# A delta-rule scan with four operations a chunk, its working tiles in SBUF, and a new order of steps around it

## What is computed

```python
x = _layernorm(x + _L0_attn_ref(...))      # causal attention, 16 heads of 8
x = _layernorm(x + _L0_ffn_ref(...))       # soft mixture of experts
x = _layernorm(x + _L1_attn_ref(...))      # gated delta rule, then a SiLU-gated MLP
x = _layernorm(x + _L1_ffn_ref(...))       # scaled ternary MLP with four layers

def step(Sm, inp):                          # delta rule, one token, per head: state 8 x 8
    qi, ki, vi, bi = inp
    Sk = jnp.einsum('bhkv,bhk->bhv', Sm, ki)
    upd = ki[..., :, None] * (vi - Sk)[..., None, :]
    Sm = Sm + bi[..., None, None] * upd
    oi = jnp.einsum('bhkv,bhk->bhv', Sm, qi)
    return (Sm, oi)
...
h = hidden_states + o @ Wo
y = rmsnorm(h, ln2)
h = h + jax.nn.silu(y @ Wg) * (y @ Wu) @ Wd
...
h = jax.nn.silu(_tlin(x, w1_w, w1_s)) * _tlin(x, w2_w, w2_s)
h = jax.nn.gelu(_tlin(h, h1_w, h1_s), approximate=False)
h = jax.nn.gelu(_tlin(h, h2_w, h2_s), approximate=False)
return _tlin(h, w3_w, w3_s)
```

## Time and profile before

| | us |
|---|---|
| runs | 1367.09, 1373.09, 1374.86; median 1373.09 |
| the profiled execution, its own time | 1367.92 |
| its span | 1366.2 |
| busy in the span: PE, DVE, ACT, POOL | 1170.0, 926.2, 623.3, 453.3 |
| the chain that ended last: PE, DVE, ACT, POOL | 50%, 25%, 10%, 4% of the span |
| HBM over the span | 57 GB/s |

### The profile page before, as it was taken

How to read it: one execution, slowest core, us unless ns; L and a number is a source line. 1 busy time by engine, 2 the same in 40 slices (tenths; PEclk the granted TensorE clock), 3 DMA queues, 4 the chain that set the end, 5 groups by cost and what they waited for, 6 DMA issues and landing times.

```text
span 1366.2 us, 19874 instructions
## 1 busy us (share of the span) xinstructions
PE 1170.0 (86%) x6173; PEld 616.5 (45%) x6173; DVE 926.2 (68%) x2401; ACT 623.3 (46%) x1194; POOL 453.3 (33%) x466
## 2 busy tenths in 40 slices
PE   5989889999899998989896751178999999999997
PEld 2434355453554544635444430134555545455453
DVE  3536536657587677776775577988988988898321
ACT  2071743736737447375373410213464454545642
POOL 3031311212333143232333233236446445544510
PEclk8999999999999999999999885579999999999999
DMA  3212030130321414114213168121020220200000
GB/s 99 82 47 71 1 109 9 48 94 33 109 65 42 131 32 134 47 29 138 55 35 67 25 149 200 48 49 44 14 65 19 47 65 8 57 24 8 24 8 8
DMA packets 85756, 79.91 MB, mean 58 GB/s; under 512 B 42800, under 2 KB 63408, under 8 KB 83632
## 3 DMA queue, kind: packets, MB, share of 16 engines
q1 hardware_dynamic: 85680, 79.01, 21.6%
HBM read 43.17 MB, written 35.00 MB: 57 GB/s over the span
## 4 chain that ended last, share of the span: by engine, by line
PE 50%; DVE 25%; ACT 10%; issue 9%; POOL 4%; DMA 1%; SPq 0%; ACTq 0%; DVEq 0%; POOLq 0%
PE ps L1305 10%; PE ps L954 5%; PE ps L1288 5%; DVE arena L1808 4%; ACT arena L1442 4%; PE ps L991 4%; PE ps L923 4%; ACT arena L1404 3%; PE ps L957 3%; PE ps L964 3%; PE ps L980 2%; DVE arena L2075 2%; PE ps L1058 2%; DVE ps L2070 2%; DVE arena L2073 2%
## 5 line engine op out<-in xcount | busy, mean ns | idle before, releaser
L1808 DVE TENSOR_REDUCE arena<-ps 128x4 f32<-128x512 f32 (+2 forms) x192 | 197.8, 1044 | 89.4 <-PE ps L957 86.3
L1305 PE MATMUL ps<-arena,late 128*128 128x512 f32 x512 | 224.5, 592 | 0.0
L1404 ACT ACTIVATE arena<-ps 128x512 f32<-128x512 f32 (+2 forms) x200 | 109.7, 567 | 232.6 <-PE ps L923 105.4
L1442 ACT ACTIVATE arena<-ps 128x1024 f32<-128x1024 f32 (+3 forms) x256 | 169.9, 711 | 30.6 <-PE ps L980 29.5
L753 POOL TENSOR_SCALAR_AFFINE_SELECT arena<-arena 128x512 f32<-128x512 f32 x128 | 82.9, 650 | 291.9 <-ACT arena L1442 290.4
L964 PE MATMUL ps<-mask_qk,ident_b 128*128 128x512 bf16 x505 | 137.6, 390 | 31.2 <-DVE arena L2087 31.1
L1305 PEld LDWEIGHTS ps<-arena,late 128*128 128x128 f32 x512 | 96.2, 190 | 115.8 <-issue 114.1
L1591 ACT ACTIVATE arena<-ps,f_s 128x512 f32<-128x512 f32 x128 | 85.2, 688 | 102.9 <-PE ps L1305 93.9
L1288 PE MATMUL ps<-arena,late 128*128 128x512 f32 x256 | 116.6, 609 | 7.8 <-ACT arena L1591 7.3
L848 POOL TENSOR_TENSOR arena<-arena 128x512 f32<-128x512 f32 x64 | 81.7, 1276 | 120.8 <-DVE slot_T L2104 76.5
L1404 ACT ACTIVATE arena<-ps,arena 128x128 f32<-128x128 f32 (+1 forms) x128 | 62.3, 528 | 124.5 <-DVE arena L1835 49.3
(11 more groups left out here) (186 smaller groups left out, 1960.7 us busy)
## 6 DMA issues: line engine op xcount, KB each, us to landing
qr<-q_rep SPq DMA_DIRECT2D x8, 1024.0 KB, 5.6
kr<-k_rep SPq DMA_DIRECT2D x8, 1024.0 KB, 7.9
scan_d<-late SPq DMA_DIRECT2D x56, 138.0 KB, 3.0
arena<-scan_d SPq DMA_DIRECT2D x12, 552.0 KB, 7.2
q_rep<-hilo SPq DMA_DIRECT2D x24, 256.0 KB, 3.3
k_rep<-hilo SPq DMA_DIRECT2D x24, 256.0 KB, 3.8
proj_d<-arena SPq DMA_DIRECT2D x8, 768.0 KB, 5.1
late<-proj_d SPq DMA_DIRECT2D x8, 768.0 KB, 4.5
```

The costliest lines, as they stand in the source:

```text
L1305: last = pe.matmul(ps[:, ring2.bank(f"{n}{c}"), :], w[:, k, c * P:(c + 1) * P], src[:, k, :], start=(k == 0), stop=(k == HC - 1))
L1404: return act.activation(dst, src(ps[:, bank, :]), func, **kw)
L1442: act.activation(prob[:, gg % 2, 2 * pr:2 * pr + 2, p_off[jt]:p_off[jt] + w], ps[:, bank:bank + 2, 0:w], ACT.Exp).then_inc(p_taken, 1)
L1808: v.tensor_reduce(heads[:, 2 * pr:2 * pr + 2, gs[0]:gs[-1] + 1], ps[:, at:at + 2, 0:len(gs) * w].rearrange("p q (n w) -> p q n w", w=w), X ...
```

## The change

1. **Four operations a chunk.** `w_s` and `k_u` become two tiles of a quarter each, with one column more: column HD of a row of `w_s` holds minus v, written by ACT ahead of time (`negate_v`, four activations of 128 elements a tile, semaphore `v_negated`); column CH of a row of `k_u` is the state. So the sum over nine terms, negated, is v minus w times state, and the sum over five is the new state. Subtraction and addition are gone.
2. **All in SBUF.** `live` is that column of `k_u` (a stride of five words) and `live_u` a tile of the arena; neither is in PSUM.
3. **Joint roots.** The root for h of one tile and that for x4 of another are taken in one sequence of eight operations on 2 x 4 values (`roots`).
4. **New order.** DVE: the sums of the second half come before `add_x4`, with two scan operations behind each; `AT_Y, AT_H, AT_X, AT_S = 4, 28, 56, 52`; in step 1 norm_x3 stands at operation 56 of the scan. ACT: `square_h` before `apply_x4`, hT's copy before those of m; in the last scan step the last history after x3T. PE: `project_o` after the first quarter of m instead of the second, `turn_h` after the third instead of the fourth, `turn_x3` after two of the four token groups of `last_out`, the three idle matmuls behind it gone; fewer idle matmuls in step 1.

The core of the diff:

```diff
-        live = [ps[:, 6 + k, 0:QUARTER * HD * HD].rearrange("p (c v d) -> p c v d", v=HD, d=HD) for k in range(2)]
-        live_u = [ps[:, 6 + k, QUARTER * HD * HD:QUARTER * HD * (HD + CH)].rearrange("p (c v j) -> p c v j", v=HD, j=CH)
-                  for k in range(2)]
+        live_u = [c2.take(QUARTER, HD, CH) for _ in range(2)]
...
+        w_s = [c2.take(QUARTER * HD, CH, HD + 1) for _ in range(2)]
+        k_u = [c2.take(QUARTER * HD, HD, CH + 1) for _ in range(2)]
+        live = [tile[:, :, :, CH].rearrange("p (c v) d -> p c v d", v=HD) for tile in k_u]
+        v_neg = [tile[:, :, :, HD].rearrange("p (c v) j -> p c v j", v=HD) for tile in w_s]
+        st_both = slot_T[:, 256:256 + 64].rearrange("p (k a b) -> p k a b", k=2, a=8)
...
+            def negate_v(t, h, q):
+
+                act.wait_ge(sc_loaded[h], CREDIT + (t - h) * 16 + 48)
+                wc = s_wu[h].rearrange("p (c j) w -> p c w j", j=CH)
+                act.activation(v_neg[q % 2], wc[:, q * QUARTER:(q + 1) * QUARTER, HD:2 * HD, :], ACT.Copy, scale=-1.0) \
+                    .then_inc(v_negated, 1)
...
-                    yield o.mark(v.tensor_reduce(now_u[:, at, :, :], w_s, X, ALU.add))
-                    yield o.mark(v.tensor_tensor(now_u[:, at, :, :], wc[:, c, :, HD:2 * HD].rearrange("p j v -> p v j"),
-                                                 now_u[:, at, :, :], ALU.subtract))
-                    yield o.mark(v.tensor_tensor(k_u, now_u[:, at, :, :].unsqueeze(2).broadcast_to([P, HD, HD, CH]),
+                    yield o.mark(v.tensor_reduce(now_u, w_s[half][:, rows, :, :], X, ALU.add, negate=True))
+                    yield o.mark(v.tensor_tensor(k_u[half][:, rows, :, 0:CH], now_u.unsqueeze(2).broadcast_to([P, HD, HD, CH]),
...
-                    yield o.mark(v.tensor_reduce(ku_sum, k_u, X, ALU.add))
...
-                    yield o.mark(v.tensor_tensor(after[:, (c + 1) % QUARTER, :, :], now[:, at, :, :], ku_sum, ALU.add))
+                    yield o.mark(v.tensor_reduce(after[:, (c + 1) % QUARTER, :, :], k_u[half][:, rows, :, :], X, ALU.add))
...
+            def roots(t, which):
+
+                o = Order(v, h_done, DVE_H, t, CREDIT)
+                rsqrt(o, which(3), which(2), which(4))
                 o.end('DVE_H')
...
-AT_Y, AT_N, AT_H, AT_S = 4, 18, 34, 84
+AT_Y, AT_H, AT_X, AT_S = 4, 28, 56, 52
...
-DVE_SCAN = 6 * NC
+DVE_SCAN = 4 * NC
```

More of the change, by code:

```diff
@@ L318, in build @@
         x2t = [c2.take(4, D) for _ in range(2)]
-        w_s = c2.take(HD, CH, HD)
-        k_u = c2.take(HD, HD, CH)
-        ku_sum = c2.take(HD, HD)
         bn2 = c2.take(4, 6)
@@ L1288, in by_hidden, with by_token @@
                 return pe.matmul(ps[:, ring2.bank(use), :], w, src, start=True, stop=True)
-            def by_token(use, turn, hid, w, done, first):
+            def by_token(use, turn, hid, w, done, first, beside=None):
                 ring2.wait_free(pe, use, *turn)
                 for j in range(4):
+                    if j == 2 and beside is not None:
+                        beside()
                     for c in range(HC):
@@ L1380, in _ @@
             now = step(0, None, 1, {})
-            now = step(1, 0, 0, now)
+            now = step(1, 0, 0, now, 2, 3)
             with pe.Fori(0, 2) as i:
@@ L1641, in keep_history, with step @@
                 act.activation(u_c[h][:, cs, :, :], live_u[q % 2], ACT.Copy).then_inc(hist_kept, 1)
-            def step(scanned, mlp, last, done, h):
+                if q < 2:
+                    negate_v(t, h, q + 2)
+                elif more:
+                    negate_v(t + 1, 1 - h, q - 2)
+            def step(scanned, mlp, last, done, h, more=True):
                 if last is not None:
@@ L1668, in step @@
                     take_n(last, 1)
-                if scanned is not None:
-                    keep_history(scanned, h, 3)
+                if scanned is not None and last is not None:
+                    keep_history(scanned, h, 3, more)
                 if last is not None:
@@ L2157, in step @@
                 further(DVE_SCAN)
-                if mlp is not None:
-                    norm_x3(mlp, 1 - h, order(ln3_done, DVE_LN, mlp, False))
+                if mlp is not None and not early_x3:
+                    norm_x3(mlp, 1 - h, Order(v, ln3_done, DVE_LN, mlp, CREDIT))
             step(0, None, None, 0)
-            step(1, 0, None, 1)
+            step(1, 0, None, 1, True)
             step(2, 1, None, 0)
```

127 lines of the change are left out of this document (70 added, 57 removed).

## The result

The changed kernel takes **1408.85 us** in the median of its runs (1407.95 to 1409.37), before it takes 1373.29: a ratio of 1.0276 (95% interval 1.0251 to 1.0301). It is slower, as forecast, but by 35.6 us and not by 10. The profiled execution has a span of 1406.7 us against 1366.2, so 40.5 us are to be explained. All of them lie in part two, which begins at 844.6 us in both, and most in the middle of it. The stretches that answer to the earlier trace rows, each from the last layer's gates to the next (ahead of the first, the start): us, PE, PEld, DVE, ACT, POOL busy, granted clock of PE, DMA, GB/s.

The account below looks back on a forecast made before the run. Part two was taken as a DVE chain to about 1262 us, then a PE chain. Terms -7.6 + 10.7 + 8 - 1.3 = +9.8 us gave 1377.7 profiled, median 1383 us; range 1380 to 1398, eight in ten 1352 to 1398.

Parts of the forecast that it names:

- The port: DVE operations with two SBUF operands contend with POOL; each long POOL operation meeting a scan multiplication costs +0.52 us.
- the stride: Scan's multiplication reading live at every fifth word: 0.10 us each, +1.6 us a step; bounds 0 and 0.17 us.
- the new wait: DVE's first-half sums, now after 13 of 16 chunks, wait 3.4 us for POOL's first pair of products.
- start, up to the first gates: Part two before the last layer's first gates: removed operations and fewer waits outweigh port and stride, -7.6 us.
- first full step: First full step of part two gives back the start's gain, 63.3 us against 52.6: +10.7 us.
- step without a scan: Step set by PE, with no fillers and no stop: -1.3 us.
- meetings: Scan multiplications on DVE meet eleven of POOL's 18 long operations: +5.7 us a step, bounds 0 and 14.
- new waits, net: DVE's waits: 3.4 us for products, 1.0 for a history copy and project_o, less 2.0 of old waits: +2.4 a step.
- the root at +19.6: DVE's root for h should end 19.6 us into the step, after 31 scan operations of 0.49 us.
- its chain of 15.9 us: From h's root through POOL, hT's transposes, layer m's last quarter and gates to the first product pair, at +35.5.
- the port hardly bites: Rival: multiplications barely meet POOL's bursts, PE becomes the bound at 51.7 us a step; about 1353 us, chance 0.24.
- the strides are free: Rival: port bites but strided reads cost nothing; middle step 54.2 us, total +4, 1377 us, chance 0.28.

Follow-up runs that it names:

- e2: Changed kernel, but the w multiplication reads 64 side-by-side constants instead of the strided state column (values wrong): 1383.76 us.
- e6: Changed kernel, but PE transposes h after layer m's last quarter, as before the change: 1403.73 us.
- e18: e14 plus x4's norm on ACT moved behind the copies of the gates; port still there: 1392.45 us.
- e17: e15 plus x4's norm on ACT moved behind the copies of the gates: 1366.51 us.
- e3: Changed kernel with u and w of the scan in PSUM (port off), ACT copying w there; state stride kept: 1379.54 us.
- e9: e3 and e6 together: u and w in PSUM, h's transposes after layer m's last quarter on PE: 1380.11 us.
- e14: e6 plus ACT's copy of hT moved back behind layer m's four copies: 1413.38 us.
- e15: e9 plus ACT's copy of hT moved back behind layer m's four copies: 1390.22 us.
- e11: e5 with h's root earlier, after 30 of 96 scan operations instead of 42: 1372.81 us.
- e10: e3 and e7 together: u and w in PSUM, h's root after 20 scan operations: 1359.44 us.
- e7: Changed kernel, but DVE takes up h's residual and joint root after 20 scan operations instead of 28: 1398.45 us.
- e5: Changed kernel with the old six-operation scan, live and u in PSUM; prices the new order alone: 1396.57 us.
- e13: e10, but in step 1 x3's norm stands behind the scan again, as before the change: 1360.42 us.
- e19: Changed kernel, but the w multiplication reads constants at hops of two words in quarters 0 and 2, four in the others: 1397.65 us.

## Why the prediction was wrong

The direction was right and the time was outside the range, 1408.9 us against 1383 and at most 1398. The port, the stride and the new wait are real, each shown above; their sizes and what they hang on were not as forecast. The sum by steps, forecast and measured:

| | forecast | measured |
|---|---|---|
| start, up to the first gates | -7.6 | +0.8 |
| first full step | +10.7 | +13.9 |
| five middle steps | +8 | +27.6 |
| step without a scan | -1.3 | -1.7 |
| end | 0 | -0.1 |
| sum | +9.8 | +40.5 |

And a middle step, by the terms of the prediction:

| | forecast | measured | from |
|---|---|---|---|
| removed operations | -8.3 | -8.3 | both are gone, forecast's own price |
| longer reductions | +1.6 | +1.5 | (452 - 427 + 488 - 418) x 16 |
| joint root | -1.0 | not taken apart | |
| meetings | +5.7 | +4.2 | 264 x 16 |
| new waits, net | +2.4 | +4.7 | 4.0 - 1.2 and 1.9 |
| stride | +1.6 | +3.3 | (627 - 418) x 16 |
| sum | +2.0 (of 53.4) | +5.5 | 59.2 - 53.7 |

With the forecast's -1.0 for the root, the measured terms add to 4.4 of the 5.5 us; part of the rest (0.7 us) is a four-element operation with two operands in SBUF (1744), 489 ns on average in place of 158 twice a step, up to 1.3 us. The new waits missed by 2.3 us in three parts. The wait for products was 4.0 and not 3.4, the one for history copies 1.9 and not 1.0. And I let 2.0 us of old waits go, from a total over part two, where the middle steps before had 1.2.

**The stride was taken at half its price: the largest single miss.** I chose 0.10 us between 0 and 0.17; it is 0.21 in these traces, and e2 shows it to be the source's hop alone. 0.11 us more on 128 multiplications is 14 us, over half of the 26 that the median lies over the forecast; as an estimate that holds, since in e2 a price of 26 us gave 25. The hop costs 0.8 ns an element. "Vector Engine (DVE) Microarchitecture Reference", 5.2 of the Trainium skill, has 1.73 against 1.05 ns a column for a source that hops 4 KiB at every element: 0.17 us by an estimate from it, nearer than my choice from the 32-element row. The upper end of the range was built on 0.17 too, so it held nothing for a late root or a longer chain.

**The step that failed beside it is the root at +19.6 and its chain of 15.9 us.** The pair was to end at +35.5 and ends at +40.3 on average, 2.8 us by the root and 2.0 by the chain. For the root I took "31 scan operations of 0.49 us"; a quiet chunk takes 2.12 us (1083.57 to 1085.69), 0.53 an operation, and meetings come on top. With the read dense the root comes at 20.7, with the port off at 20.2: its lateness is stride and port once more, through DVE's list. In the chain, "the last quarter of m 3.4" took 4.8 to 6.1 us, because PE ran part of it at 1.2 GHz behind its own stop. That stop was forecast, at 2 us, and nothing was put for what follows it.

That chain was longer than before by plan, with the quarter in it, and taking the quarter out doesn't bring the old 13.6 us back (e6), which the working could not have told: nothing in it followed ACT's list. There x4's norm waits for the joint root, and layer m's copies and two table loads stand behind it. I had costed the negations on ACT and never the *order* there. Three moves together, h's transposes on PE, hT's copy on ACT and x4's norm on ACT, took 16 us off the changed kernel (e18) and 13 with the port off (e17 against e3). Of them the transposes alone gave 5 or nothing (e6, e9), hT's copy on top cost 10 (e14 against e6, e15 against e9), and x4's norm on top gave 21 and 24. x4's norm moved alone was not tried, nor were the joint roots parted again in the new order, so whether that one move would do stays open. An earlier root also helps: 24 us with the old scan (e11), 20 with the port off (e10 against e3), 10 in the changed kernel (e7).

**The start was forecast 7.6 us shorter and came 0.8 longer.** The stride explains 3.5 us of it (32 multiplications more dearly by 0.11). The rest is not taken apart. The first gates come at 945.0 in the changed kernel (forecast: 937), at 943.0 with the root earlier (e7), 941.2 with the read dense (e2), 939.4 with the port off (e3); with the old scan at 945.1 and, with the root earlier, 938.8 (e5, e11).

**The port's size was right in part by luck.** 5.7 us forecast and 4.2 measured looks like a good term. But I priced it as a constant: eleven long operations met, whatever the rest does. Over the kernels in which both multiplications can meet POOL it ran from 4.2 to 9.1 us a step, and it was small in the changed one because DVE stood beside the burst. The rule of the Trainium skill ("SBUF — State Buffer", Who interferes with whom) holds here: with one operand of each in PSUM the 256 multiplications of e3 show no meeting.

**What else held and what didn't.** The step without a scan, the end and the reductions came as forecast. The first full step grew by 13.9 us, not 10.7, but it had no early start to give back; with the port off and the root earlier, 6 us of its length came from x3's place (e13). Of the signs named, DVE's idle (3.4 us) came, and PE's before h's transposes was 3.8 us, not 2. The maximum of a multiplication was 1.74 us, not 1.3. POOL's output products hardly grew, 1302 ns on average over the span against the 1400 that I had put; its gate products took 1366 and 1330 where they had taken 1274 and 1271.

Some of the working's sums are off by little. The chain's terms add to 15.6 and not 15.9 us, 55.4 less 53.7 is 1.7 and not 1.6, the step without a stride price is 53.8 and not 54.2, and 1373 - 21 is 1352.

The rival *the port hardly bites* was priced at 1353 us. e3 is nearest to that case, with the stride and ACT's extra copies: 1379.5, no faster than before, so taking the port away would not have done what the rival says. Only with the root earlier as well does it come to 1359 (e10). The rival *the strides are free* was priced at 1377 us; e2 gives 1383.8.

## What to carry to other kernels

Terms that share one cover don't add. Where an engine can either wait out another's burst or run through it and collide, removing one cost buys the other; measure each part alone *and* both together, since here 29 and 10 us alone made 49. When two results are computed together, look on every engine at what is queued behind the consumer of the one that was not urgent: with x4's norm moved out of the front of ACT's list the chain was 4.6 us shorter (18.8 in e15, 14.2 in e17), more than the 1.0 us that I had expected of the joint root. And keep an operand that is read every few words out of the short chain, or price it from a row with the hop, not between a bound and zero.

## What the runs showed of the hardware

- **A hop of five words costs ScalarE as well.** The history copy of 256 elements took 384 ns from dense PSUM (the first row, before) and 666 from the strided column in SBUF (the second, changed). Two things changed there. The dense copy of u beside it, 128 elements, went from 272 only to 302 when its source moved to SBUF, so my estimate is that over 0.2 us are the hop.

```profile
L1640 ACT ACTIVATE arena<-ps x32: 375/384/415, 861.2 to 1259.0; 128x256 f32<-128x256 f32 x32
```

```profile
L1647 ACT ACTIVATE arena<-arena x32: 646/666/687, 868.5 to 1301.2; 128x256 f32<-128x256 f32 x32
```

- **The collision is mostly DVE's.** POOL's 512-element product kept its median (1268 ns, 1275 before) and its mean is 1302 (gate products 1366 and 1330), while a DVE multiplication that met one went up to 1740 from 627. On average DVE's two multiplications of a chunk lost 264 ns.
- **The hop costs nearly the same with the other operand in PSUM**: 610 ns in e3, 0.19 us over the dense 420 of before. And it has a threshold between two and four words (e19).
- **A stop can cost PE more than its length**: behind one of 3.8 us the next eight records took 1.2 us more, at a granted clock of 0.74. It need not: in e3 stops of 2.8 us were followed twice by 3.60 us at a clock of 1.00 (1081.28 and 1249.43), and one of 2.2 us by 5.30 us at 0.67 (1025.08).
